# Order of a step's first half in a fused attention and feed-forward kernel: both row tiles' queries and keys first, then the values

## The reference

```python
x = x + tanh(g_xattn) * xattn(layernorm(x), ctx, ctx, mask, ...)
x = x + tanh(g_ffn) * ffn(layernorm(x), ...)
# ffn, for each of 2 layers (8 heads of 64, window 128, hidden 682):
h = shift_token(x); q, k, v = split(h @ wqkv)        # 256 -> 3 x 512
q = l2norm(q) * qs; k = l2norm(k) * ksc; q, k = rotary_xpos(q, k)
x = x + local_attention(q, k, v) @ wo
h = layernorm(shift_token(x)) * lg + lb
a, g = split(h @ w1 + b1); x = x + (a * gelu(g)) @ w2 + b2
```

## Time and profile before

| | |
|---|---|
| time, median of 3 runs | 847.18 us (847.17 to 848.62) |
| profiled execution, its own time | 846.62 us |
| its span | 844.8 us |
| TensorE busy (matmul) | 759.1 us, 90% of the span |
| VectorE busy | 569.6 us, 67% |
| ScalarE busy | 502.4 us, 59% |
| GpSimd busy | 441.6 us, 52% |
| DMA, mean busy share | 14.0% of 16 engines (the data queue) |

### The profile page before, as it was taken

How to read it: one execution, slowest core, us unless ns; L and a number is a source line. 1 busy time by engine, 2 the same in 40 slices (tenths; PEclk the granted TensorE clock), 3 DMA queues, 4 the chain that set the end, 5 groups by cost and what they waited for, 6 DMA issues and landing times. The chain is left out here.

```text
span 844.8 us, 17684 instructions
## 1 busy us (share of the span) xinstructions
PE 759.1 (90%) x5088; PEld 652.9 (77%) x5088; DVE 569.6 (67%) x1675; ACT 502.4 (59%) x1241; POOL 441.6 (52%) x625
## 2 busy tenths in 40 slices
PE   5988777989999999999998988999999999999977
PEld 4877655887878787878786877878787878787856
DVE  2798896385858584848485856757575858585842
ACT  2333436366767666666667573757575757575742
POOL 1333464373838383838383645737373737373722
PEclk9999987799999999999999998999999999999999
DMA  7344323151000000000000001010101010101000
GB/s 212 128 137 149 110 57 131 26 219 37 3 29 9 29 8 26 12 20 17 19 18 19 20 2 50 2 51 0 50 0 50 0 50 0 50 0 37 1 26 13
DMA packets 31156, 38.34 MB, mean 45 GB/s; under 512 B 7356, under 2 KB 21776, under 8 KB 31120
## 3 DMA queue, kind: packets, MB, share of 16 engines
q1 hardware_dynamic: 31120, 37.90, 14.0%
HBM read 29.51 MB, written 8.39 MB: 45 GB/s over the span
## 5 line engine op out<-in xcount | busy, mean ns | idle before, releaser
L1351 POOL TENSOR_SCALAR pr<-pr,rl 128x128 f32<-128x128 f32 (+1 forms) x256 | 106.4, 429 | 96.9 <-DVE rl L1129 96.8
L840 ACT ACTIVATE pr<-sm,nb,rn 128x128 f32<-128x128 f32 (+1 forms) x256 | 137.3, 539 | 19.3 <-DVE nb L1124 19.2
L415 PE MATMUL ps<-hT_hi,w_hi 128*128 128x256 f32 (+1 forms) x384 | 110.9, 289 | 1.4 <-DVE hT_lo L1091 1.4
L1120 DVE CUSTOM_DVE_ANT_0 sm<-ps,wmask 128x128 f32<-128x128 f32 (+1 forms) x256 | 81.4, 355 | 41.6 <-PE ps L581 23.0
L415 PE MATMUL ps<-hT_hi,w_lo 128*128 128x256 f32 (+1 forms) x384 | 108.3, 282 | 0.0
L415 PE MATMUL ps<-hT_lo,w_hi 128*128 128x256 f32 (+1 forms) x384 | 107.9, 281 | 0.0
L1314 POOL TENSOR_TENSOR rn<-ss,nhalf 128x16 f32<-128x16 f32 x32 | 95.3, 2978 | 3.7 <-POOL ss L1310 2.0
L798 ACT ACTIVATE sqb<-ps 128x512 f32<-128x512 f32 x64 | 38.2, 598 | 84.9 <-PE ps L415 84.9
L415 PE MATMUL ps<-wqkv_hi,yT_hi 128*128 128x512 f32 x192 | 79.8, 416 | 8.7 <-DVE arena L967 5.3
L1257 POOL TENSOR_SCALAR hrs<-hmv 128x2 f32<-128x2 f32 x16 | 3.1, 193 | 151.7 <-DVE hmv L1145 151.7
L809 ACT ACTIVATE gl<-ps,b_sb 128x256 f32<-128x256 f32 x96 | 45.5, 474 | 53.3 <-PE ps L415 52.9
(11 more groups left out here) (146 smaller groups left out, 2209.2 us busy)
## 6 DMA issues: line engine op xcount, KB each, us to landing
arena<-x SPq DMA_DIRECT2D x16, 256.0 KB, 3.6
ystream<-arena SPq DMA_DIRECT2D x16, 256.0 KB, 2.0
y_next<-ystream SPq DMA_DIRECT2D x16, 256.0 KB, 2.9
y_res<-ystream SPq DMA_DIRECT2D x16, 256.0 KB, 2.6
arena<-L_ffn_w SPq DMA_DIRECT2D x2, 1364.0 KB
arena<-ctx SPq DMA_DIRECT2D x8, 256.0 KB, 4.1
arena<-mask_BxSxS_ik SPq DMA_DIRECT2D x8, 256.0 KB, 2.9
xmid<-arena SPq DMA_DIRECT2D x8, 256.0 KB, 2.0
```

Source lines behind the costliest of these rows:

```text
L415: last = mm(out, lhsT(a), rhs(b), start=(start and i == 0), stop=(stop and i == 2))
L840: A(pr[:, h % NS, a:b], sm[:, h % NS, a:b], ACT.Exp, bias=nb[:, h, t:t + 1], scale=rn8[:, t, h:h + 1], accum_out=ls[:, h, t:t + 1]).then_i ...
L1120: V.tensor_tensor_reduce(sm[:, h % NS, a:b], bank(h % NS)[:, a:b], wmask[:, a:b], 1.0, NEG, ALU.add, ALU.max, mx[:, h, t:t + 1]).then_inc( ...
L1351: G.tensor_scalar(pr[:, h % NS, a:b], pr[:, h % NS, a:b], rl[:, h, t:t + 1], 1.0, ALU.mult, ALU.mult).then_inc(pn_done, 1)
```

## The change

Three streams get a new order in a step's first half; no instruction is added or removed.

- TensorE: before, queries, keys and values of tile 0, then the queries of tile 1, the feed-forward transposes, the keys and the values of tile 1. After, queries and keys of tile 0, queries and keys of tile 1, the values of tile 0, the feed-forward transposes, the values of tile 1.
- ScalarE: the four squares come first, then the copy of tile 0's values, `hT_hi`, the copy of tile 1's values, and only then the table load and the first two GELUs. Before, tile 1's values were copied between the first and the second GELU.
- VectorE: `rotate_sin(0)` comes before `low_hT` instead of behind it, and `add_queries(0)` behind the norms of tile 1 instead of ahead of them.

```diff
--- before.py
+++ after.py
@@ -640,16 +640,15 @@
                 if first:
                     transpose_probs(NB - 1)
                 if A:
+                    project(1, (0, 1))
                     project(0, (2,))
                 if first:
                     weigh_values(NB - 1)
-                if A:
-                    project(1, (0,))
                 if F:
                     pe.wait_ge(hn_done, s)
                     transpose_rows(hn, 7).then_inc(h_tr, 1)
                 if A:
-                    project(1, (1, 2))
+                    project(1, (2,))
                 if F:
                     up(0)
                     up(1)
@@ -855,19 +854,17 @@
                 if la is not None:
                     squares(0, 0)
                     squares(0, 1)
+                    squares(1, 0)
+                    squares(1, 1)
                     values(0)
                 if lf is not None:
                     act.wait_ge(h_tr, s)
                     wait(act, up_mm, HC * f)
                     A(hT[0][:], halves(7), ACT.Copy).then_inc(hT_high, 1)
                 if la is not None:
-                    squares(1, 0)
-                    squares(1, 1)
+                    values(1)
                 if lf is not None:
                     gelu(0)
-                if la is not None:
-                    values(1)
-                if lf is not None:
                     gelu(1)
                     high_u(0)
                 if la is not None:
@@ -1167,14 +1164,13 @@
                     dve.wait_ge(w_ready, FIRST)
                 if A:
                     rotate_cos(0)
+                    rotate_sin(0)
                 if F:
                     low_hT()
                 if A:
-                    rotate_sin(0)
-                    add_queries(0)
-                if A:
                     norms(1, 0)
                     norms(1, 1)
+                    add_queries(0)
                 if F:
                     gated(0)
                 if A:
```

## The result

The changed kernel takes 852.07 us (median of 9 runs, 848.55 to 853.81); the kernel before took 846.89 us beside it (9 runs, 844.56 to 848.62). The ratio, of the means, is 1.0057, with a 95% interval of 1.004 to 1.0075: slower, by 5.2 us between the medians. The profiled execution took 852.39 us with a span of 850.6 us, against 846.62 and 844.8 before.

What follows compares the result with a forecast made beforehand. TensorE, by far the busiest engine, loses time only through waits. Steps 2-7 and 10-14 +5.7, 8 and 15 +0.4, 1 and 9 -1.05, 0 +0.4: +5.4 us, forecast 852.5; 8-in-10 range 849 to 858.

Steps and rivals of the forecast that it cites:

- The wait for the bank: TensorE at tile 1's values: waits for ScalarE's copy of tile 0's values out of the shared bank, 0.59 us a step.
- the second limit: At `up(0)`: without the bank wait, hT's late low part would cost about 0.35 us.
- The two don't add: The late low part of hT costs 0 under cover of the 0.59 us bank wait, about 0.35 without it.
- hT in time: VectorE's low part of hT is there 0.26 us ahead of `up(0)`, before the change 1.19; cost 0.
- The table load: ScalarE ahead of the first GELU: 1.28 us, now exposed, GELU 0.55 late on top of 0.60; dies out, 0.02 set aside.
- The tail: VectorE, addition of tile 1's queries to end of key scaling: 3.01 to 2.91 us; 0.10 back, 0.44 in steps 1, 8, 15.
- The two collisions: In VectorE's tail: GpSimd's low parts 2 and 3 still stretch two of its three instructions, giving 2.91 us.
- The lock rival: GpSimd's power (2.93 us) holds VectorE's scaling of tile 0's keys: 1.6 us a step, 876 us; chance 0.04.
- The special steps: Steps 1 and 9, shorter waits for late-normalised rows: -0.7 and -0.35 us; step 0, addition of tile 0's queries: +0.4; step 16 unchanged.

Runs made afterwards that it cites:

- e4: The changed kernel with the feed-forward transposes ahead of both tiles' values, hT's high part ahead of both copies, bank still shared; 862.35 us, ratio 1.0191.
- e1: The changed kernel with tile 1's values in PSUM bank 6 instead of tile 0's bank 2; 850.12 us, ratio 1.0036.
- e5: The changed kernel with tile 1's values in bank 6 and the transposes and hT's high part moved as in e4; 844.98 us, ratio 0.9981.
- e2: The changed kernel with ScalarE copying tile 1's values between the first two GELUs again, as before; 852.73 us, ratio 1.0065.
- e7: The kernel before with VectorE's new order alone; 845.44 us, ratio 0.9987.
- e3: The changed kernel with VectorE's old order, TensorE and ScalarE as changed; 859.24 us, ratio 1.0153.
- e10: e3 with GpSimd's addition of the bias b2 moved to the very start of the step; 857.86 us, ratio 1.0128.
- e9: e5 with tile 1's values copied between the first and the second GELU, as before; 865.69 us, ratio 1.0226.
- e8: e3 with GpSimd's addition of the bias b2 moved behind the last low part of the hidden layer; 866.55 us, ratio 1.0241.

## Why the prediction was right

852.5 was forecast, 852.07 measured.

**The wait for the bank** was worked out as 0.59 and is 0.58; e4 gives the same arithmetic with the cover taken away, 0.94. e1 and e5 show that it is the cause: the bank and the transposes together take the loss away, 42.42 against 42.99. In e1, the bank alone, the second limit that the prediction named (0.35) takes its place at 0.33. "The two don't add" held.

**hT in time.** The low part was to be there 0.26 ahead of `up(0)`; it ends at 573.60 + 0.69 = 574.29, 0.35 ahead of 574.64. Cost 0, as forecast.

**The table load** costs 1.28, and not 1.79: the GELU follows at 1.30. Its lateness of 1.09 in all was forecast as 1.15, and that it dies out is shown by e2 and e5. The 0.02 set aside for it was not needed: the third GELU is 0.56 later than before against the shift product (13.58, before 13.02), less than `up(0)`.

**The tail** was forecast at 2.91 and is 2.97, so 0.04 came back and not 0.10. The two collisions that it counted are there, but on the first and the third instruction. The step's sum is then 0.59 at the tail's start (582.29 - 565.96 = 16.33, before 15.74), less 0.04 or 0.05: 0.54, where 0.52 was forecast. In steps 1, 8 and 15 the first addition is stretched as in the others now, 0.38 back where 0.44 was forecast. e7 finds the same small gain without the rest of the change.

**The lock rival** (0.04) is refuted by the scaling of tile 0's keys: it started at 577.66, inside a power that ran from 576.30 for 2.93, and took 0.68.

**The special steps** hold the mis-sized terms. Step 1 gained 0.35 and not 0.7. Its two causes were sized about right: the low part is 0.85 later against the last `hn` (0.9 forecast) and the tail 0.38 shorter. But `up(0)` came only 0.06 earlier against the shift product and not 0.25 (9.42 behind it, before 9.48), because the last `hn` itself came 0.30 later against it (6.04, before 5.74). The row statistics wait there for VectorE's split of weights, which ends at the same absolute time in both traces (167.18 and 167.15) though step 1 began 0.25 earlier. In step 9 `up(0)` came 0.27 earlier (0.25 forecast), and the tail gave 0.03 back instead of 0.10. In step 0 I had let VectorE's addition pay; GpSimd's paid, and its next power came 0.51 later, where 0.4 was forecast. The table's -0.25 isn't this term: 0.47 were gained ahead of it, in the cross-attention, and 0.29 behind it, neither of which the change explains. The end was 0.35 longer, which I had not forecast and have not explained.

So the hit to 0.4 us is in part luck. The errors cancel: eleven steps by 0.55 give 6.0 (5.7 forecast), steps 8 and 15 0.31 (0.4), steps 1 and 9 -0.62 (-1.05), everything ahead of step 1 -0.25 (+0.4), the end +0.35 (0): 5.8 against 5.4. Outside the ordinary steps each of these comes from one trace of each kernel and is no larger than what the traces differ by there. What the experiments show is the ordinary step: 0.54 measured, 0.52 forecast.

What stays open: why, behind one and the same wait, the granted clock falls in one trace and not in another, or at another place. In step 7 TensorE waits 2.56 us for the split weights before the change, after it, and in e1, e3 and e7 alike; the clock of step 7 is 1.00 in the first two, where it falls only about the end of the step, and 0.96 to 0.97 in the others. Such stretches are part of the long step 7 of e3 and of step 9 of e4 and e10.

## What to carry to other kernels

When two products share a PSUM bank, count what the tensor engine has to do between the last matmul of one and the first of the other: here the handover takes 0.52 + 0.60 + 0.06 = 1.18 us from the start of the last matmul (to the copy, the copy, the release), and whatever isn't filled is paid in each step. Give the second product another bank only after listing who uses that one next, and who releases it: e5 has the bank without the loss, and e9, with a single copy moved, loses 19 us to the kernel before. Judge such a reordering by the ordinary steps; single runs scatter by as much as the effect. And measure in each trace from a point just ahead of the place: step 0's cost of 0.51 can't be seen in absolute times.

## What the runs showed of the hardware

- A GpSimd addition of 128x512 stretches even the smallest VectorE instructions that fall beside it: a 128x2 product from 0.16 to 1.28 us, a 42x256 cast from 0.28 to 0.98. The Trainium skill, "SBUF — State Buffer", section "Who interferes with whom", has the rule that a VectorE instruction with two SBUF inputs and a GpSimd instruction that reads SBUF exclude each other for their whole length; for the product, which reads two tiles in SBUF, the trace agrees, down to this size. The cast reads only one, and the rule in these words doesn't cover it; that it is held too is what e3, e8 and e10 show. What counts is where a short instruction on the critical path falls, not how much the two engines overlap.
- GpSimd's power (128x16, 2.93 us) does not do this. VectorE's scaling of keys, with two SBUF inputs, took 0.68 inside it, at 577.66 in the changed kernel. Here the measurement differs from that rule, and the measurement decides.
- Behind a table load of 1.28 us the function started 1.30 behind its start, in e5 as in the changed kernel. The drain of about 1.38 that the Trainium skill, "ScalarE: Activation LUTs", section "What ACT_TABLE_LOAD costs", adds to each switch does not show.
- A block of 512-wide matmuls begun behind transposes or a wait needs about 0.1 us more for its first one: the second follows after 0.31 to 0.34 us, the others after 0.23 (e4, and the changed kernel at 573.13).
- Behind a long wait of TensorE the granted clock can fall to its lower level: 0.50 (1.2 GHz) in e4 from 531.04 to 537.04 behind a wait of 2.51 us. Behind a wait of 2.49 at the same place in the kernel before it stayed at 1.00.
